# Gate weights of chunks 4 to 10 turned by transposing transfers instead of TensorE

## The reference

```python
def cond(x, c, weight, c_weight, bias):       # x (128, 32, 512)
    out = conv1d(x, weight, padding=4, taps=9, groups=4)
    return out + (c @ c_weight.T)[:, :, None] + bias[None, :, None]

def ffn(x, W_gate, W_up, W_down):             # gate, up (1376, 512); down (512, 1376)
    xt = x.reshape(-1, 512)                   # 4096 tokens
    return (silu(xt @ W_gate.T) * (xt @ W_up.T) @ W_down.T).reshape(x.shape)

y = x + ffn(cond(x, cond_128, weight, c_weight, fside_S_0), W_gate, W_up, W_down)
```

## Time and profile before

| | |
|---|---|
| time of the runs, median of three | 736.04 us |
| the profiled execution's own time | 736.35 us |
| its span | 734.5 us |
| granted TensorE clock | 0.998 |
| TensorE matmul busy | 723.2 us (98%) |
| VectorE busy | 454.0 us (62%) |
| ScalarE busy | 291.4 us (40%) |
| GpSimd busy | 81.5 us (11%) |
| chain that ended last, by engine | TensorE 93%, VectorE 2%, DMA 1% |
| read from HBM, written | 103.47 MB, 34.34 MB |

### The profile page before, as it was taken

The page is one execution under the profiler, slowest core; times in us unless marked ns, Lnnn a source line. Parts: engine busy times, 40 slices in busy tenths (PEclk is TensorE's granted clock), DMA queues, the critical chain, the costliest instruction groups (busy, mean ns, idle before and its releaser), DMA issues.

```text
span 734.5 us, 10005 instructions
## 1 busy us (share of the span) xinstructions
PE 723.2 (98%) x3288; PEld 590.1 (80%) x3288; DVE 454.0 (62%) x711; ACT 291.4 (40%) x523; POOL 81.5 (11%) x119
## 2 busy tenths in 40 slices
PE   7999999999999999999999999999999999999997
PEld 6777888868888888877888888887888888887886
DVE  3888998969746787736626878745744333334223
ACT  3665656648634334334422333424421333333221
POOL 4543544423100000000000000000000000000000
PEclk9999999999999999999999999999999999999999
DMA  6696786769979887666437987765444966764403
GB/s 185 118 310 244 245 279 219 257 150 262 298 258 301 234 238 219 203 209 173 149 102 246 261 239 203 216 214 157 153 134 135 299 197 187 199 192 153 145 28 115
DMA packets 121365, 149.25 MB, mean 203 GB/s; under 512 B 21634, under 2 KB 59682, under 8 KB 121314
## 3 DMA queue, kind: packets, MB, share of 16 engines
q1 hardware_dynamic: 120544, 148.27, 67.5%
q10 hardware_dynamic: 770, 0.34, 0.3%
HBM read 103.47 MB, written 34.34 MB: 188 GB/s over the span
## 4 chain that ended last, share of the span: by engine, by line
PE 93%; DVE 2%; DMA 1%; SPq 1%; issue 1%; ACT 1%; POOL 0%; ACTq 0%; DVEq 0%; POOLq 0%
PE bank L802 55%; PE bank L865 33%; PE bank L710 3%; SPq L368 1%; DMA x_in<-in_x 1%; PE bank L676 1%; PE bank L724 0%; DMA stage<-g_all 0%; PE bank L733 0%; DVE hc_lo L1196 0%; PE bank L744 0%; PE bank L719 0%; DVE g_all L1448 0%; DVE ring L1196 0%; DVE xt_lo L1196 0%
## 5 line engine op out<-in xcount | busy, mean ns | idle before, releaser
L802 PE MATMUL bank<-hc_hi,ring 128*128 128x512 f32 (+1 forms) x1204 | 373.6, 391 | 0.5 <-DVE ring L1196 0.5
L802 PEld LDWEIGHTS bank<-hc_hi,ring 128*128 128x128 f32 (+1 forms) x1204 | 221.4, 185 | 49.8 <-DVE ring L1196 0.7
L802 PE MATMUL bank<-hc_lo,ring 128*128 128x512 f32 (+1 forms) x602 | 234.8, 390 | 0.0
L865 PE MATMUL bank<-ring,g_hi 128*128 128x512 f32 (+1 forms) x704 | 217.7, 390 | 1.5 <-DVE ring L1196 1.5
L936 ACT ACTIVATE mix<-bank 128x512 f32<-128x512 f32 (+1 forms) x129 | 77.0, 597 | 245.3 <-PE bank L802 245.3
L865 PEld LDWEIGHTS bank<-ring,g_hi 128*128 128x128 f32 (+1 forms) x704 | 131.7, 188 | 30.6 <-DVE g_lo L1196 2.8
L865 PE MATMUL bank<-ring,g_lo 128*128 128x512 f32 (+1 forms) x352 | 137.0, 389 | 0.0
L802 PEld LDWEIGHTS bank<-hc_lo,ring 128*128 128x128 f32 (+1 forms) x602 | 111.5, 185 | 25.6
L1196 DVE TENSOR_TENSOR g_lo<-g_all,g_hi 128x512 fp32r<-128x512 f32 x88 | 62.8, 717 | 90.1 <-ACT g_hi L936 90.1
L936 ACT ACTIVATE g_hi<-g_all 128x512 fp32r<-128x512 f32 x88 | 54.9, 629 | 115.8 <-PE bank L865 114.8
L865 PEld LDWEIGHTS bank<-ring,g_lo 128*128 128x128 f32 (+1 forms) x352 | 66.1, 188 | 14.0
(11 more groups left out here) (133 smaller groups left out, 497.0 us busy)
## 6 DMA issues: line engine op xcount, KB each, us to landing
ring<-saved SPq DMA_DIRECT2D x297, 256.0 KB, 3.0
saved<-ring SPq DMA_DIRECT2D x99, 256.0 KB, 3.1
g_all<-in_x SPq DMA_DIRECT2D x32, 256.0 KB, 3.7
out_y<-g_all SPq DMA_DIRECT2D x32, 256.0 KB, 3.4
stage<-win SPq DMA_DIRECT2D x96, 64.0 KB, 3.0
x_in<-in_x SPq DMA_DIRECT2D x72, 68.0 KB, 3.0
w_nat<-in_L_ffn_W_gate SPq DMA_DIRECT2D x10, 256.0 KB, 3.8
w_nat<-in_L_ffn_W_up SPq DMA_DIRECT2D x10, 256.0 KB, 3.9
```

The lines of the kernel that those rows point to most:

```text
L802: mm = pe.matmul(bank[0:w, :], wt, hv, start=fresh and q == 0 and t == 0, stop=q == 1 and t == 2, skip_group_check=not fresh)
L865: mm = pe.matmul(acc(half, tt)[:], gs, wd, start=f == 0 and t == 0, stop=f == FC - 1 and t == 2)
```

## The change

For chunks 3 to 9 (the fourth to the tenth) TensorE's turn of the gate chunk is left out. GpSimd copies the low and the high 16 bits of each number of the gate chunk into `gate_halves` (after `wrap` of the chunk), SyncE issues one transposing transfer into `gate_crossing`, and ScalarE joins the halves into `x_gate` where it copied the PSUM bank before. Both buffers lie in the last chunk of `g_all` and exist once; the waits that follow from this are written out. The crossing of chunk f+1 is issued within `save_products(f)`, ahead of the save of kind 3 and behind the stage step. Chunks 0, 1, 2 and 10 and all up chunks are turned as before.

```diff
+        CROSSED_GATES = range(3, FC - 1)
+        gate_halves, gate_crossing = (g_all[:, FC - 1, half, :].bitcast(U16) for half in range(2))
+
+        def gates_turned(f):
+            return f + 1 - len([n for n in CROSSED_GATES if n <= f])
...
             def load_nat(f):
                 w = width(f)
                 for kind in range(2):
-                    if 2 * f + kind >= NNAT:
-                        sp.wait_ge((gate_turned, up_turned)[kind], f - NNAT // 2 + 1)
+                    used = f - NNAT // 2
+                    if used >= 0 and kind == 0 and used in CROSSED_GATES:
+                        sp.wait_ge(gate_halved, used - CROSSED_GATES[0] + 1)
+                    elif used >= 0 and kind == 0:
+                        sp.wait_ge(gate_turned, gates_turned(used))
+                    elif used >= 0:
+                        sp.wait_ge(up_turned, used + 1)
...
+            def cross_gate(f):
+                n = f - CROSSED_GATES[0]
+                sp.wait_ge(gate_halved, n + 1)
+                if n > 0:
+                    sp.wait_ge(gate_kept, f)
+                sp.dma_start_transpose(out=gate_crossing.rearrange("p (j f) -> p j f", f=P), in_=gate_halves).then_inc(gate_crossed, LD)
...
                     if kind == K_S1 and 1 <= f - 1 - lag(0) <= STEPS:
                         stage_step(1, f - 2 - lag(0))
+                    if kind == K_S1 and f + 1 in CROSSED_GATES:
+                        cross_gate(f + 1)
                     sp.wait_ge(w_made[kind], f + 1)
                     save_slot(product_at(0, f, kind))
...
+            def halve_gate(f):
+                n = f - CROSSED_GATES[0]
+                pool.wait_ge(nat_wrapped, 2 * f + 1)
+                if n == 0:
+                    pool.wait_ge(hc_done[K_S3], hc_count(0))
+                else:
+                    pool.wait_ge(gate_crossed, LD * n)
+                numbers = w_nat[:, 2 * f % NNAT, PAD:PAD + L].bitcast(U16)
+                pool.tensor_copy(gate_halves.rearrange("f (h c) -> f h c", h=2),
+                                 numbers.rearrange("f (c h) -> f h c", h=2)).then_inc(gate_halved, 1)
...
                     if g == 0 and f + 2 < FC:
                         wrap(f + 2)
+                    if g == 0 and f + 2 in CROSSED_GATES:
+                        halve_gate(f + 2)
...
                     product(g, f, 4)
-                    if g == 0 and f + 2 < FC:
+                    if g == 0 and f + 2 < FC and f + 2 not in CROSSED_GATES:
                         turn_gate(f + 2)
...
                 if part == 0:
-                    act.wait_ge(gate_turned, f + 1)
+                    if f in CROSSED_GATES:
+                        act.wait_ge(gate_crossed, LD * (f - CROSSED_GATES[0] + 1))
+                    else:
+                        act.wait_ge(gate_turned, gates_turned(f))
...
-                    hi(x_gate[:, :, 0:w], gate_ps[:].rearrange("p (i f) -> p i f", i=KC)[:, :, 0:w]).then_inc(gate_kept, 1)
+                    if f in CROSSED_GATES:
+                        hi(x_gate[:].rearrange("p i f -> p (i f)").bitcast(U16).rearrange("p (c h) -> p c h", h=2),
+                           gate_crossing.rearrange("p (h c) -> p c h", h=2)).then_inc(gate_kept, 1)
+                    else:
+                        hi(x_gate[:, :, 0:w], gate_ps[:].rearrange("p (i f) -> p i f", i=KC)[:, :, 0:w]).then_inc(gate_kept, 1)
```

More of the change, by code:

```diff
@@ L222, in adaln_ffn @@
         down_turned = sem("down_turned")
+        gate_halved = sem("gate_halved")
+        gate_crossed = sem("gate_crossed")
         down_halved = sem("down_halved")
@@ L401, in load_down @@
                 else:
-                    sp.wait_ge((gate_turned, up_turned)[f % 2], FC - 1 + f // 2)
+                    last = FC - 2 + f // 2
+                    if f % 2 == 1:
+                        sp.wait_ge(up_turned, last + 1)
+                    elif last in CROSSED_GATES:
+                        sp.wait_ge(gate_halved, last - CROSSED_GATES[0] + 1)
+                    else:
+                        sp.wait_ge(gate_turned, gates_turned(last))
                 sp.dma_start(down_nat(f)[:, :, 0:w], w_down[:, f * P:f * P + w].rearrange("(q d) f -> d q f", d=P)
                              ).then_inc(down_loaded[f % NDOWN], LD)
+            def cross_gate(f):
[4 more added lines that the diff above has]
+                sp.dma_start_transpose(out=gate_crossing.rearrange("p (j f) -> p j f", f=P), in_=gate_halves).then_inc(gate_crossed, LD)
             def cross_down(f):
@@ L1085, in split_g @@
                         act.wait_ge(w_made[kind], FC)
-                    act.wait_ge(gate_turned, FC)
+                    act.wait_ge(gate_turned, gates_turned(FC - 1))
                     act.wait_ge(up_turned, FC)
```

## The result

The changed kernel takes 744.56 us at the median of four runs (743.72 to 745.18) against 736.15 (735.78 to 736.65): ratio 1.0114, 95% interval 1.0102 to 1.0126: slower by 1.1%. Its profiled execution has a span of 741.9 us against 734.5, and the kernel run once more beside later experiments gave 744.82, ratio 1.0111 (1.0091 to 1.0130), span 744.1. Two of the five executions of e5, at mean granted clocks of 0.85 and 0.56, took 805.14 and 1212.73 us and are left out of its ratio.

A forecast was written before the change was run, and what follows sets the result against it. TensorE was taken to set the pace in the first group; five rounds of 13.0 us through late crossings, plus 1.4 at the start, less 57.8, gave +8.6 on 736.35: 744.95, less 0.31 for the median, 744.7 us; range 738 to 750.

The forecast's parts named there:

- D(0): Moment VectorE has read convolution step 0 of the second group, 76.85 us before the change; D(k) likewise for step k.
- P: Length of one of five rounds from D(k) to D(k+1) through the late crossing: 13.0 us, against TensorE's 11.0.
- Stage issues: Term of P: SyncE's four stage-step transfers issued ahead of the crossing, taken as 2.8 us a round.
- Landing: Term of P: a crossing from issue to landing, taken as 3.8 us, from rows of 3.1 to 5.2.
- Join to D: Terms of P: ScalarE's join to the K_S4 split's end, 2.19 us, then VectorE to its read's end, 4.12.
- The start, s: Delay of D(0) itself from chunk 3's crossing landing late: 1.4 us, ends 0 and 2.1.
- The shift of (8,4): Delay of product (8,4), the last one hit, on TensorE: 5P + s - 57.8 = +8.6 us, removed turns included.
- What was hidden: Added work claimed free: seven GpSimd copies covered by idle time, ScalarE's join 0.58 us longer, no port cost in the new place.
- Rival 1: Crossings land in time and TensorE stays the bound: 733.3 us at best; chance 7%.
- Rival 2: Crossings land as quickly as saves, 2.9 us: P = 12.1, +2.7, 739.1 us; chance 18%.
- rival 3: Longer rounds from SyncE's queue backing up, landings of 4.2, VectorE and GpSimd meeting: P = 14.8, 754.6 us; chance 8%.
- Rival 4: Lateness doesn't add up since VectorE catches up; product (f,4) 0.6 us late, once: 737.0 us; chance 5%.

The follow-up runs named there:

- e5: Changed kernel with the crossing issued still behind the wait for VectorE's convolution read but ahead of the four stage issues; ratio 1.0057.
- e9: Same kernel as e5, run again for an undisturbed trace; 739.88 us, ratio 1.0056.
- e7: Changed kernel with only chunks 3 and 4 crossed, the others turned on TensorE; 736.54 us, ratio 1.0005.
- e4: Changed kernel with copies of halves and crossings made but unused: TensorE turns every chunk, ScalarE copies from the bank; 735.76 us, ratio 0.9991.
- e1: Changed kernel with the crossing of chunk f+1 issued at the head of the saves of chunk f, ahead of the first save; 733.55 us, ratio 0.9963.
- e8: Changed kernel with only chunks 6 and 8 crossed, behind the stage step as there; 736.61 us, ratio 1.0010.
- e11: Same kernel as e6, run again beside e10 on the same chip; 740.50 us, ratio 1.0054.
- e6: Changed kernel with only chunks 5, 7 and 9 crossed behind the stage step, the others turned on TensorE; 739.64 us, ratio 1.0048.
- e10: Kernel of e6 plus four TensorE transposes of the identity, result unused, for each crossed chunk; 739.58 us, ratio 1.0051.
- e3: Changed kernel plus four TensorE transposes of the identity, result unused, for each crossed chunk where the turn was; 742.88 us, ratio 1.0084.

## Why the prediction was right, step by step

**The forecast** was 744.7 us at 62%; measured 744.56. The mechanism is the one predicted. That the number is so near is luck: one term of the round was priced too long, one was missing, and they nearly cancel. For the profiled execution the sum gave 744.95, and that took 743.72.

**The round.** From D(0) = 77.20 in the profile after: D(1) 89.41, D(2) 102.51, D(3) 116.44 (its stage step starts at 116.47), D(4) 128.59, and (8,4) at 139.11, 10.52 behind D(4), which is a fifth round of 13.94 less the 3.42. Five rounds are 12.21 + 13.10 + 13.93 + 12.15 + 13.94 = 65.3 us, 13.07 each, against P = 13.0.

- Stage issues: 2.52, 3.45, 2.79, 2.49, 3.20, mean 2.9, priced at 2.8: 0.5 more over five rounds.
- Landing: 3.13, 3.10, 4.05, 3.11 and 3.11 in the five rounds, mean 3.3, priced at 3.8 (bounds 3.1 to 5.2). Mis-sized, 2.5 too long over five rounds. I had taken the DMA share of a whole iteration (0.70); in the microsecond ahead of the five issues it is 0.51, 0.27, 1.0, 0.33 and 0.60, and the one at 1.0 is chunk 7's, which took the 4.05 (105.97 to the join at 110.02). The first two crossings, issued at shares of 1.1 and 1.0, took 4.15 (54.95 to the join at 59.10) and 4.3.
- Join to D: 82.99 to 89.41 is 6.42, 96.10 to 102.51 is 6.41, priced at 2.19 + 4.12 = 6.31: 0.5 more over five rounds.
- Not in my sum: in the two rounds with x loads SyncE gets to the stage step 0.57 and 1.28 us after the read, 1.85 together. I had taken the stage step's start for D in all five, though the earlier trace rows has the last two stage steps 12.5 us apart. e9 shows this bound by itself. Together: -2.5 + 0.5 + 0.5 + 1.85 = +0.3, which is the 65.3 against my 65.0.
- What hands the lateness on: D lies 3.57 us behind the start of the (f,4) that waited, in all five rounds, where before it lay 2.4 behind it. VectorE follows ScalarE's join now, no longer TensorE.

**The start, s.** 1.4 priced, 0.35 measured (77.20 against 76.85; 0.66 from the first mark). The crossing of chunk 3 took 4.15 instead of 4.5 and was issued 0.4 us sooner against the first mark. e7 has the two first crossings alone, with their two turns less, at +0.4 us (-0.4 to +1.1).

**The shift of (8,4).** 65.3 + 0.35 - 57.8 = 7.9, forecast 8.6. That 139.11 - 131.2 gives 7.9 too is no test, since the fifth round was worked out from (8,4). Nothing is given back behind it.

**What was hidden, and stayed so.** GpSimd's copy (mix_t behind it still waited 1.9 us or more for T2), the port, the issue and the traffic: e4. The join's 0.58: e1.

**What went.** 3.1 us were forecast for the case that the crossings land in time. e1 got 2.7 of them. "All on the path" was too much: from the first long run of matmuls to the first step of the next group's convolution, which waits for VectorE, e1 takes 24.3 us with the turns of chunks 3 and 4 gone, and before 24.1. From there to the first down product it takes 83.2 against 85.2: 2.0 us for five turns of 0.44. Rival 1 was wrong for this kernel and right for its neighbour with two lines moved. **Rival 2** (crossings as quick as saves) had the landing nearly right, at 3.1 (median) against the 2.9 of the earlier trace rows, but not its time of 739.1: chunk 7's landing, the stage issues and SyncE's lateness made the round 13.07 instead of 12.1. (Its time, and that of rival 3, leave out the 0.31 us that the forecast takes off.) **Rival 3** (longer rounds) is out: one landing reached 4.05, the stage issues 3.45 at most, and GpSimd's copies met no VectorE work. The rule of the Trainium skill ("Advanced Engine Details and Errata", X-Bar Transpose (TRN2)), that transposing transfers are as fast as regular ones, agrees with this trace from 75 to 141 us: 3.1 us to landing, beside 3.0 for the 256 KB saves. It doesn't agree from 50 to 68 us (4.2 beside 2.8), nor in e9 (6.3 and 5.8 beside 3.6 and 3.0), nor for the issue (1.26 us here, a save's about 0.5). **Rival 4** (the lateness doesn't add up) is refuted by e8 against the changed kernel, for chunk 6 by the gap itself, for chunk 8 by the terms of the two gaps, which only happen to be of one size. Not forecast at all: the stretches at 1.2 GHz, worth 0 or about 1.5 us by where they fall.

## What to carry to other kernels

A transfer that replaces an engine's work has to be issued a whole flight (here 3 to 4 us, up to 6 in a full queue) before its reader's turn; look for what stands ahead of it in the issuing engine's program, waits and issues alike, before pricing the work it saves. If the wait ahead of it depends on what its reader releases, the flight is paid every round; and the issuing queue's own length per round is a second bound, to be added up separately. When such a change loses, try its transfers in an earlier place before taking it back: here two lines, moved, turned +1.1% into -0.4%.

## What the runs showed of the hardware

- A transposing transfer of 128 x 1024 two-byte elements within SBUF took 1.26 us to issue and landed 3.1 us after its issue began in the four rounds of the changed kernel in which the DMA engines had been busy for 0.27 to 0.60 of the microsecond ahead, and 4.05 in the one in which they were full. Behind the x loads of e9, at shares of 0.9 and 1.0, the issue took 2.48 and 2.85 us, and it landed after 6.3 and 5.8. The share alone doesn't decide: at 1.0 ahead of it another crossing of e9 took 1.32 to issue and 5.25 to land, and in e4 one issued right behind a stage step (91.19) took 2.29 to issue.
- TensorE fell to 1.2 GHz for some 3.5 us behind gaps of 1.96 us (after, at 100.4), 3.10 (its second trace, at 140), 2.13 (e11, at 112.2), 2.54 (e6, at 135.7) and 3.03 (e9, at 110), and did not behind gaps of 2.88 (after, at 139.11), 2.45 (its second trace, at 113.58), 2.36 (e10, at 134.83) and 2.21 (e3, at 112.66). The size of the gap alone doesn't decide. On the path the stretch cost 1.4 us (second trace) and 1.6 (e6 against e11). In the first trace it lay inside a round that the landing set: that round's terms, 0.57 + 2.79 + 4.05 + 6.42 and 0.1 between them, make its 13.93 us without it.
